# Two-chunk layout of gate and up weights, wider low-rank products, and a new order of the first rounds

## The chip, the cores and the metric

The kernel runs on one core of a Trainium2 chip. The metric is device microseconds of one execution. TensorE multiplies, VectorE, ScalarE and GpSimd do elementwise work, and SyncE (SP in the profile) issues most transfers from the chip's memory. The engines run their own instruction streams in order and meet at semaphores.

## The reference

Input x is 2 x 512 tokens of 512 features. What is computed, in four stages:

```
q, k, v = lin(x, Wq), lin(x, Wk), lin(x, Wv);  x1 = x + lin((q + k + v) / 3, Wo)
h = silu(lin(x1, Wgate)) * lin(x1, Wup)          # 1792 wide
x = layernorm(x + x1 + lin(h, Wdown))
x = layernorm(x + x @ W.T + low-rank)            # a 512 x 512 layer
x = layernorm(x + attention(x))                  # one head of 128
x = layernorm(x + expert mix(x))                 # 64 experts of rank 16, best 16 taken
```

Here lin(x, W) is x @ W.T plus a low-rank product x @ A.T @ B.T of rank 16. The weights of the first two stages come as 4-bit codes with a scale for each block of 64, and are looked up in a table of 16 values.

## The kernel before

**Weights.** The codes are read in 62 chunks of 128 x 512 (CHUNKS). For each chunk ScalarE and VectorE evaluate the table as a maximum and minimum of straight lines: `low` (two ScalarE passes into `bent` and a PSUM bank, one VectorE pass), `mid` (one and one), `clip` (VectorE), `out` (ScalarE L856 or L834, then VectorE into `value`, then GpSimd multiplies by the scale into `wf`, L745). TensorE makes the low-rank product A.T @ B.T of the chunk (the function `lora`), VectorE adds it to `wf` (`merge`, L1418 or L1415), and `split` writes the chunk as a high part rounded to the matmul type (ScalarE, `gu_hi` or `wd_hi`, L826) and a low part with what is left (GpSimd, `gu_lo` or `wd_lo`, L786).

**Products.** Every matrix product is made of three matmuls: high x high, high x low, low x high (`product`, L1056). A unit is one gate or one up product of 512 tokens with a chunk of 128 outputs: four k-steps of three matmuls, twelve in all.

**Rounds.** The 1792 hidden features are 14 rounds f of 128. A round has gate and up for each half of the tokens (units 2f and 2f + 1), then the products with the down chunk, which are made for pairs of rounds and spread over later rounds. The chunks g, u and d of round f + 1 are prepared during round f; in rounds 6, 8, 10 and 12 a chunk of the next stage's layer (an f chunk) is prepared as well. `silu`, `h` (the product with up, on VectorE), and `hsplit` (high part on ScalarE, low part on GpSimd) follow each unit.

**Order.** The order of the vector engines' work is one list, `vector_order`, and each of VectorE, ScalarE and GpSimd walks it and does its own share. From round 2 on it is made by a loop with the table BEATS; before that it is written out. TensorE's order is another list, `tensor_order`; in round f it is gate, down, up, down for the first half and the same for the second, with the `lora` of coming chunks between. A `lora` waits until the merge of the chunk before it has been done, since all use one PSUM bank.

**Gate and up chunks before.** Chunk g of a round holds the gate weights for all 512 input rows, chunk u those of up. `unit` waits for the chunk that it uses, once, before its twelve matmuls. The low-rank product of a chunk is four matmuls of 128 columns, one for each 128 input rows (L1069).

**Low-rank factors.** They are stacked three times over the partitions, and `bprep` rewrites a part of the stack as low parts: ScalarE picks rows (`chosen`, L830), GpSimd subtracts (L774). Part 0 is the A side; parts 1 and 2 are the B side for rounds 0 to 3 and 4 to 13. `dprep` does the same for the down chunks, `fprep` for the f chunks. The DMA of the B side is issued by SyncE with the attention chunks, between the codes.

Of the kernel before, what the change touches and what calls it, by code (L numbers as in the profile page):

```python
# [24 lines left out]
P = 128  # L25
# [81 lines left out]

BEATS = {0: [0] * 8, 4: [1, 0, 1, 0, 1, 0, 1, 0], 6: [1, 0, 1, 1, 2, 0, 1, 0], 8: [2, 0, 2, 0, 2, 0, 2, 0]}

# [21 lines left out]
RING_LN = 4  # L131
LB_FIRST = 4
XSPLIT_AFTER = [6, 7, 8, 9, 11, 12, 13, 14]


def vector_order():
# [67 lines left out]
    alone(("g", 1), 0)  # L204
    order.append(("x1", 0))
    alone(("g", 1), 1)
    order += [("merge", ("g", 0)), ("split", ("g", 0)), ("x1", 1), ("x1", 2), ("x1", 3)]
    order += [("merge", ("u", 0)), ("split", ("u", 0))]
    alone(("u", 1), 0)
    order.append(("x1", 4))  # L210
    alone(("u", 1), 1)
    order += [("merge", ("g", 1)), ("x1", 5), ("split", ("g", 1))]
    alone(("d", 0), 0)
    order.append(("x1", 6))
    alone(("d", 0), 1)
    order += [("merge", ("u", 1)), ("x1", 7)]
    alone(("d", 1), 0)
    order += [("split", ("u", 1)), ("dprep", 0)]
    alone(("d", 1), 1)
    order.append(("silu", 0))  # L220
    unit_h(0)
    half(("g", 2), 0)
    order += [("merge", ("d", 0)), ("split", ("d", 0)), ("bprep", 2), ("silu", 1)]
    unit_h(1)
    half(("g", 2), 1)
    order += [("merge", ("d", 1)), ("split", ("d", 1))]
    for f in range(1, NF):
        downs = downs_beside(f) + [None] * 4
        ahead = [(m, f + 1) for m in "gud" if (f, m) != (1, "g")] if f < NF - 1 else []
# [105 lines left out]
def build(nc, codes, scales, scales_qkv, eye, stack_low, xT, loA_o, loB_o, loA_qkv, loB_qkv, loA_gu, loB_gu,  # L335
          loA_d, loB_d, loA_f, loB_f, w_qkv, b_qkv, w_o, b_o, ex_A, ex_B, w_r, out):
    with ExitStack() as ctx:
# [32 lines left out]
        rows = at("rows", 98, [P, TT, H])  # L370
        bgu_raw = at("bgu_raw", 98, [P, FF])
        agu_raw = at("agu_raw", 105, [P, 2, 512])
        wq_hi = at("wq_hi", 146, [P, KT, H], F32R)
# [4 lines left out]
        wd_lo = at("wd_lo", 124, [P, RING_H, H], F32R)  # L378
        la_gu = at("la_gu", 134, [P, 2, 512], F32R)
        x1_hi = at("x1_hi", 146, [P, KT, TOK], F32R)  # L380
        x1_lo = at("x1_lo", 162, [P, KT, TOK], F32R)
        gu_hi = at("gu_hi", 178, [P, RING_GU, 2, KT, P], F32R)
        gu_lo = at("gu_lo", 186, [P, RING_GU, 2, KT, P], F32R)
# [4 lines left out]
        lb_gu = at("lb_gu", 194, [P, FF], F32R)  # L388
        la_d = at("la_d", 30, [P, FF // 2])
        la_dp = at("la_dp", 94, [P, FF // 2], F32R)  # L390
# [6 lines left out]
        half_eye = at("half_eye", 202.5, [P, P])  # L397
        three_eye = at("three_eye", 138, [P, P])

# [193 lines left out]

        def lb_cut(i):
            return slice(0, LB_FIRST * P) if i == 1 else slice(LB_FIRST * P, FF)

# [26 lines left out]
        def dest(c):  # L623

            kind, k = c
            if kind in "gu":
                g = "gu".index(kind)
                return gu_hi[:, k % RING_GU, g, :, :], gu_lo[:, k % RING_GU, g, :, :]
            if kind == "d":
                return wd_hi[:, k % RING_H, :], wd_lo[:, k % RING_H, :]  # L630
            return wff_hi[:, k, :], wff_lo[:, k, :]

        def shaped(c, w):
            return w.rearrange("p (k o) -> p k o", k=KT) if c[0] in "gu" else w

# [23 lines left out]
        def _(sp):  # L659
# [3 lines left out]
            for j, c in enumerate(CHUNKS):  # L663
# [3 lines left out]
                if c == ("v", 1):  # L667
                    sp.dma_start(bgu_raw[:, :], loB_gu).then_inc(bgu_in, 16)
                    sp.dma_start(agu_raw[:, :, :], loA_gu).then_inc(agu_in, 16)
                if c == ("q", 3):  # L670
                    sp.dma_start(xs[:, :, SEQ:], xT[:, :, SEQ:]).then_inc(x_in, 16)
                if c == ("k", 2):
                    sp.dma_start(la_d[:, :], loA_d).then_inc(lorad_in, 16)
                    sp.dma_start(lb_d[:, :, :], loB_d).then_inc(lorad_in, 16)
                    sp.dma_start(low_rows[:, 1:6], stack_low).then_inc(lorad_in, 16)
                if c == ("g", 3):
                    sp.wait_ge(x1_ready, NB * KT)
                    sp.dma_start(la_f[:, :], loA_f).then_inc(loraf_in, 16)
                    sp.dma_start(lb_f[:, :], loB_f).then_inc(loraf_in, 16)
# [37 lines left out]
        def _(pool):  # L717
# [7 lines left out]
            for item in filter(None, V):  # L725
# [41 lines left out]
                elif kind == "bprep":  # L767
                    i = item[1]
                    pool.wait_ge(bprep_hi, i + 1)
                    if i == 0:  # L770
                        lo, raw = la_gu[:, :, :], agu_raw[:, :, :]
                    else:
                        lo, raw = lb_gu[:, lb_cut(i)], bgu_raw[:, lb_cut(i)]
                    pool.tensor_tensor(lo, raw, lo.bitcast(F32), ALU.subtract).then_inc(bprep_done, 1)  # L774
                elif kind == "dprep":
# [48 lines left out]
        def _(act):  # L824
# [14 lines left out]
            for item in filter(None, V):  # L839
# [65 lines left out]
                elif kind == "bprep":  # L905

                    i = item[1]
                    act.wait_ge(bgu_in, 16)
                    act.wait_ge(agu_in, 16)
                    act.wait_ge(lorad_in, 48)  # L910
                    if i == 0:
                        chosen(la_gu[:, :, :], agu_raw[:, :, :], low_rows[:, 4:5], bprep_hi)
                    else:
                        cut = lb_cut(i)
                        chosen(lb_gu[:, cut], bgu_raw[:, cut], low_rows[:, 5:6], bprep_hi)
                elif kind == "dprep":
# [11 lines left out]
                elif kind == "down" and not item[1]:  # L928
                    t = item[2]
                    act.wait_ge(down_ready, t + 1)  # L930
                    act.wait_ge(bprep_done, 3)
                    copy(rows[:, t, :], down_bank(0, t)[:, :], down_added)
                elif kind == "silu":
                    n = item[1]
                    act.wait_ge(gate_ready, n + 1)
                    if n == 0:
                        act.wait_ge(dprep_done, 1)
                    if n >= 2:
# [111 lines left out]
        def _(pe):  # L1050
# [9 lines left out]
            def lora(c):  # L1060
# [84 lines left out]
            for n in range(KT, NB * KT):  # L1145
# [465 lines left out]
def laid_out(a):  # L1611
# [11 lines left out]
    for kind, k in CHUNKS:  # L1623
# [6 lines left out]
        elif kind in "gu":  # L1630
            g = "gu".index(kind)
            codes.append(cg[g][cut].reshape(P, KT, P).transpose(2, 1, 0).reshape(P, H))
            scales.append(sg[g][cut].reshape(P, KT, 2).transpose(2, 1, 0).reshape(2, H))
# [66 lines left out]
```

## Time and profile before

| | |
|---|---|
| median of three runs | 529.33 us (527.44 to 530.64) |
| profiled execution | 527.05 us, of which its span is 525.2 us |
| busy share of the span | TensorE 93%, VectorE 70%, ScalarE 56%, GpSimd 51% |
| mean granted clock of TensorE | 0.997 of full |
| gate and up products | 672 matmuls, 89.4 + 88.0 + 87.9 us busy |
| low-rank products of g and u chunks | 112 matmuls, 15.9 us busy |

Busy times of matmuls overlap, since one starts before the one ahead has ended; what a matmul costs is the step from its start to the start of the next. A row of the timeline has start, duration, engine, line, operation, what is written and read, shape and count, and in brackets how long the engine had been idle and what ended that. PE is TensorE's matmuls, PEld its weight loads, DVE VectorE, ACT ScalarE, POOL GpSimd.

### The profile page before, as it was taken

How to read it: one execution, taken by the hardware profiler on the slowest of the kernel's cores; microseconds unless marked ns; L12 is line 12 of the kernel's file. 1: busy time of each engine (PE TensorE's matmuls, PEld its weight loads, DVE VectorE, ACT ScalarE, POOL GpSimd, SP SyncE). 2: the span in 40 equal slices, each digit the busy share in tenths (PEclk: the TensorE clock that was granted, in tenths of full speed). 3: DMA queues.
4: the chain of work that ended last, by engine and by line, in shares of the span. 5: the costliest groups of instructions: out<-in, count | busy, mean ns of one | idle time of the engine just before them, and what ended most of it. 6: DMA issues, size and time to landing. Idle time of an engine off the chain costs nothing.

```text
span 525.2 us, 7548 instructions
## 1 busy us (share of the span) xinstructions
PE 485.9 (93%) x2272; PEld 392.1 (75%) x2272; DVE 366.1 (70%) x704; ACT 293.7 (56%) x542; POOL 267.1 (51%) x261
## 2 busy tenths in 40 slices
PE   2479889889999999999999999899998899999996
PEld 1246578668878888888888888688886688888884
DVE  5989878655458787997997974577457866366433
ACT  6989757655666566574765742158487422333021
POOL 4787726954446666575765653247479410110001
PEclk9999999989999999999999999999999999999999
DMA  8674412422223243343342300740000000000011
GB/s 208 227 246 138 136 60 85 137 81 81 61 80 101 81 121 100 102 108 93 109 126 72 117 1 3 267 162 1 1 1 1 2 0 22 21 20 21 1 41 40
DMA packets 21416, 43.01 MB, mean 82 GB/s; under 512 B 3329, under 2 KB 3457, under 8 KB 21121
## 3 DMA queue, kind: packets, MB, share of 16 engines
q1 hardware_dynamic: 21152, 42.16, 25.5%
q0 software_dynamic: 224, 0.38, 0.4%
q8 instruction: 19, 0.31, 0.2%
q14 instruction: 21, 0.16, 0.1%
HBM read 40.42 MB, written 2.10 MB: 81 GB/s over the span
## 4 chain that ended last, share of the span: by engine, by line
PE 76%; issue 6%; ACT 5%; DVE 5%; POOL 2%; DVEq 0%; ACTq 0%
PE bank L1056 66%; PE bank L1211 3%; PE bank L1069 2%; PE bank L1315 1%; PE bank L1116 1%; POOL gu_lo L786 1%; ACT bent L834 1%; PE bank L1104 1%; ACT prob L1012 1%; DVE wf L1418 1%; DVE value L1394 1%; PE bank L1194 1%; ACT bank L834 1%; PE bank L1078 1%; PE bank L1113 0%
## 5 line engine op out<-in xcount | busy, mean ns | idle before, releaser
L745 POOL TENSOR_TENSOR wf<-value,scale 128x512 f32<-128x512 f32 x50 | 64.5, 1291 | 73.7 <-DVE value L1394 70.4
L1056 PE MATMUL bank<-x_hi,gu_hi 128*128 128x512 f32 x224 | 89.4, 399 | 2.7 <-POOL gu_lo L786 2.7
L1056 PE MATMUL bank<-x_lo,gu_hi 128*128 128x512 f32 x224 | 88.0, 393 | 0.0
L1056 PE MATMUL bank<-x_hi,gu_lo 128*128 128x512 f32 x224 | 87.9, 392 | 0.0
L809 POOL TENSOR_TENSOR rstd<-veps,neg_half 128x1 f32<-128x1 f32 x32 | 17.6, 550 | 120.8 <-issue 109.6
L834 ACT ACTIVATE bank<-code 128x512 f32<-128x512 int32 x124 | 68.7, 586 | 0.0
L1372 DVE SCALAR_TENSOR_TENSOR low<-bent,bank 128x512 f32<-128x512 f32 x62 | 42.4, 684 | 25.5 <-ACT bank L834 22.1
L792 POOL TENSOR_TENSOR h_lo<-act_f,h_hi 128x512 fp32r<-128x512 f32 x28 | 36.5, 1302 | 36.3 <-ACT h_hi L826 36.3
L1056 PEld LDWEIGHTS bank<-x_hi,gu_hi 128*128 128x128 f32 x224 | 42.5, 190 | 11.5 <-issue 3.5
L1056 PEld LDWEIGHTS bank<-x_hi,gu_lo 128*128 128x128 f32 x224 | 42.5, 190 | 9.1
L1056 PEld LDWEIGHTS bank<-x_lo,gu_hi 128*128 128x128 f32 x224 | 42.5, 190 | 8.0
L1385 DVE SCALAR_TENSOR_TENSOR low<-low,bank 128x512 f32<-128x512 f32 x62 | 42.6, 687 | 5.7
L1056 PE MATMUL bank<-wd_hi,h_hi 128*128 128x512 f32 x112 | 44.9, 401 | 1.6 <-DVE rows L1461 1.6
L1378 DVE SCALAR_TENSOR_TENSOR bank<-code,bank 128x512 f32<-128x512 int32 x62 | 42.6, 687 | 5.1 <-ACT bank L856 4.7
L826 ACT ACTIVATE h_hi<-act_f 128x512 fp32r<-128x512 f32 x28 | 17.7, 631 | 50.9 <-DVE act_f L1454 45.5
L1056 PE MATMUL bank<-wd_hi,h_lo 128*128 128x512 f32 x112 | 43.8, 391 | 0.0
L1056 PE MATMUL bank<-wd_lo,h_hi 128*128 128x512 f32 x112 | 43.7, 390 | 0.0
L1461 DVE TENSOR_TENSOR rows<-bank,rows 128x512 f32<-128x512 f32 x40 | 27.6, 689 | 21.5 <-PE bank L1056 21.2
L1394 DVE SCALAR_TENSOR_TENSOR value<-bank,low 128x512 f32<-128x512 f32 x62 | 42.4, 684 | 0.1
L834 ACT ACTIVATE bent<-code 128x512 f32<-128x512 int32 x62 | 38.4, 620 | 3.7 <-DMA code<-codes 3.7
L786 POOL TENSOR_TENSOR gu_lo<-wf,gu_hi 128x512 fp32r<-128x512 f32 x28 | 36.3, 1296 | 4.5 <-ACT gu_hi L826 4.2
L856 ACT ACTIVATE bank<-code 128x512 f32<-128x512 int32 x62 | 36.7, 591 | 2.6 <-DVE low L1385 2.6
(202 smaller groups left out, 1152.0 us busy)
## 6 DMA issues: line engine op xcount, KB each, us to landing
code<-codes SPq DMA_DIRECT2D x62, 256.0 KB, 2.7
scale<-scales SPq DMA_DIRECT2D x100, 128.0 KB, 3.0
xs<-xT SPq DMA_DIRECT2D x2, 1024.0 KB, 6.0
ea_raw<-ex_A SPq DMA_DIRECT2D x1, 2048.0 KB, 10.0
eb_raw<-ex_B SPq DMA_DIRECT2D x1, 2048.0 KB, 7.6
out<-rows SPq DMA_DIRECT2D x8, 256.0 KB, 2.0
bgu_raw<-loB_gu SPq DMA_DIRECT2D x1, 896.0 KB, 5.9
wqkv_raw<-w_qkv SPq DMA_DIRECT2D x1, 768.0 KB, 4.3
```

The costliest lines, as they stand in the source:

```text
L745: pool.tensor_tensor(w, v, scale[:, i % RING_CODES, :], ALU.mult).then_inc(scaled_done, 1)
L786: pool.tensor_tensor(lo, shaped(c, w), hi.bitcast(F32), ALU.subtract).then_inc(lo_done, 1)
L792: pool.tensor_tensor(h_lo[:, f % RING_H, hs], act_f[:, n % 2, :], h_hi[:, f % RING_H, hs].bitcast(F32), ALU.subtract).then_inc(hlo_done, 1)
L826: nc.scalar.activation(dst, src, ACT.Copy).then_inc(done, 1)
L834: nc.scalar.activation(dst, src, ACT.Prelu, bias=float(start), scale=float(slope), alpha=float(alpha)).then_inc(done, 1)
L856: nc.scalar.activation(mid_ps[:, :], code[:, j % RING_CODES, :], ACT.Relu, bias=float(RELU_MID[1]), scale=float(RELU_MID[0])).then_inc(mid ...
L1056: last = nc.tensor.matmul(ps, a, b, start=start and i == 0 and n == 0, stop=stop and i == len(terms) - 1 and n == 2)
L1372: nc.vector.scalar_tensor_tensor(low[:, j % 2, :], bent[:, j % 2, :], float(BEND_LOW[3] - BEND_LAST[3]), last_ps[:, :], ALU.add, ALU.min). ...
L1378: nc.vector.scalar_tensor_tensor(mid_ps[:, :], code[:, j % RING_CODES, :], float(CODE_SHIFT), mid_ps[:, :], ALU.add, ALU.max).then_inc(mid ...
L1385: nc.vector.scalar_tensor_tensor(lj, lj, float(BEND_LAST[3]), mid_ps[:, :], ALU.add, ALU.min)\
L1394: nc.vector.scalar_tensor_tensor(value[:, j % 2, :], top_ps[:, :], float(BEND_TOP[3]), low[:, j % 2, :], ALU.add, ALU.max).then_inc(value_ ...
L1461: nc.vector.tensor_tensor(rows[:, t, :], down_bank(gi, t)[:, :], rows[:, t, :], ALU.add)\
```

## The change

A gate/up chunk now holds gate and up side by side, for half of the input rows: chunk g of a round has k-steps 0 and 1 of both, chunk u k-steps 2 and 3. A unit waits for both chunks, the second one after half of its matmuls. With the B side of gate and up side by side (and zero where the other's rows stand), one low-rank matmul makes 256 columns, both outputs of one k-step, and a chunk takes two instead of four. The A side has half the columns and the B side twice as many, so it comes in two transfers and is prepared in four parts; the parts use a buffer of their own for the rounded values. Some buffers move (`la_d` no longer shares room with `act_f`, and a wait of the first `silu` for `dprep` goes). The written-out order of the rounds 0 and 1 and of the second half of x1 is changed; the loop from round 2 on stays, and so does `tensor_order`. TensorE makes the low-rank product of ("g", 1) and ("u", 1) one x1 product later.

```
-BEATS = {0: [0] * 8, 4: [1, 0, 1, 0, 1, 0, 1, 0], 6: ..., 8: ...}
+BEATS = {0: [0] * 8, 6: ..., 8: ...}
-LB_FIRST = 4
+LB_PARTS = [(0, 4), (4, 7), (7, 11), (11, NF)]
+LB_HALF = 7
...
     order += [("bprep", 1), ("m1", KT - 1)]
     alone(("g", 1), 0)
-    order.append(("x1", 0))
+    order += [("x1", 0), ("x1", 1)]
     alone(("g", 1), 1)
-    order += [("merge", ("g", 0)), ("split", ("g", 0)), ("x1", 1), ("x1", 2), ("x1", 3)]
-    order += [("merge", ("u", 0)), ("split", ("u", 0))]
+    order += [("merge", ("g", 0)), ("x1", 2), ("split", ("g", 0)), ("x1", 3), ("merge", ("u", 0)), ("split", ("u", 0))]
     alone(("u", 1), 0)
-    order.append(("x1", 4))
+    order += [("bprep", 2), ("x1", 4)]
     alone(("u", 1), 1)
-    order += [("merge", ("g", 1)), ("x1", 5), ("split", ("g", 1))]
+    order += [("merge", ("g", 1)), ("x1", 5), ("bprep", 3), ("split", ("g", 1))]
     alone(("d", 0), 0)
     order.append(("x1", 6))
     alone(("d", 0), 1)
-    order += [("merge", ("u", 1)), ("x1", 7)]
-    alone(("d", 1), 0)
-    order += [("split", ("u", 1)), ("dprep", 0)]
-    alone(("d", 1), 1)
+    order += [("merge", ("u", 1)), ("x1", 7), ("dprep", 0), ("split", ("u", 1))]
+    alone(("d", 1))
+    order.append(("bprep", 4))
     order.append(("silu", 0))
-    unit_h(0)
-    half(("g", 2), 0)
-    order += [("merge", ("d", 0)), ("split", ("d", 0)), ("bprep", 2), ("silu", 1)]
-    unit_h(1)
-    half(("g", 2), 1)
-    order += [("merge", ("d", 1)), ("split", ("d", 1))]
-    for f in range(1, NF):
+    alone(("g", 2), 0)
+    order += [("h", 0), ("hsplit", 0)]
+    alone(("g", 2), 1)
+    order.append(("silu", 1))
+    alone(("u", 2), 0)
+    order += [("merge", ("d", 0)), ("split", ("d", 0)), ("h", 1), ("hsplit", 1)]
+    alone(("u", 2), 1)
+    order += [("merge", ("d", 1)), ("silu", 2), ("split", ("d", 1))]
+    alone(("d", 2), 0)
+    order += [("merge", ("g", 2)), ("split", ("g", 2)), ("h", 2), ("hsplit", 2)]
+    half(("d", 2), 1)
+    order += [("merge", ("u", 2)), ("silu", 3), ("split", ("u", 2))]
+    unit_h(3)
+    for f in range(2, NF):
...
                 if c == ("v", 1):
-                    sp.dma_start(bgu_raw[:, :], loB_gu).then_inc(bgu_in, 16)
-                    sp.dma_start(agu_raw[:, :, :], loA_gu).then_inc(agu_in, 16)
+                    sp.dma_start(agu_raw[:, :], loA_gu).then_inc(agu_in, 16)
+                    sp.dma_start(bgu_raw[0][:, :, :, :], loB_gu[:, :LB_HALF, :, :]).then_inc(bgu_in, 16)
...
+                if c == ("v", 3):
+                    sp.dma_start(bgu_raw[1][:, :, :, :], loB_gu[:, LB_HALF:, :, :]).then_inc(bgu_in, 16)
...
                 elif kind == "bprep":
...
-                        chosen(lb_gu[:, cut], bgu_raw[:, cut], low_rows[:, 5:6], bprep_hi)
+                        act.wait_ge(bprep_done, i)
+                        chosen(lb_part(i)[2], lb_part(i)[1], low_rows[:, 5:6], bprep_hi)
...
-                    if n == 0:
-                        act.wait_ge(dprep_done, 1)
...
-                    pe.wait_ge(bprep_done, 2 if k < LB_FIRST else 3)
-                    for h in range(KT):
-                        last = nc.tensor.matmul(lora_ps[:, h * P:(h + 1) * P],
-                                                la_gu[:, "gu".index(kind), h * P:(h + 1) * P],
-                                                lb_gu[:, k * P:(k + 1) * P], start=True, stop=True)
+                    pe.wait_ge(bprep_done, 2 + next(i for i, (a, b) in enumerate(LB_PARTS) if a <= k < b))
+                    for h in range(2):
+                        m = 2 * "gu".index(kind) + h
+                        last = nc.tensor.matmul(lora_ps[:, 2 * h * P:2 * (h + 1) * P], la_gu[:, m * P:(m + 1) * P],
+                                                lb_gu[k // LB_HALF][:, k % LB_HALF, :, :], start=True, stop=True)
...
-                if r in (0, 2):
-                    lora((("g", 1), ("u", 1))[r // 2])
+                if r in (1, 2):
+                    lora((("g", 1), ("u", 1))[r - 1])
...
-                pe.wait_ge(hi_done, split_no(("gu"[g], f)))
-                pe.wait_ge(lo_done, split_no(("gu"[g], f)))
                 s, ps = f % RING_GU, unit_ps[m % 3][:, :]
-                product(ps, [(gu_hi[:, s, g, k, :], gu_lo[:, s, g, k, :], x1_hi[:, k, tk], x1_lo[:, k, tk])
-                             for k in range(KT)]).then_inc((gate_ready, unit_ready)[g], 1)
+                for h in range(2):
+                    pe.wait_ge(hi_done, split_no(("gu"[h], f)))
+                    pe.wait_ge(lo_done, split_no(("gu"[h], f)))
+                    last = product(ps, [(gu_hi[:, s, k, g, :], gu_lo[:, s, k, g, :], x1_hi[:, k, tk], x1_lo[:, k, tk])
+                                        for k in (2 * h, 2 * h + 1)], start=h == 0, stop=h == 1)
+                last.then_inc((gate_ready, unit_ready)[g], 1)
```

## Rows read from the trace of the kernel before

**Rows 1.** Busy time by stretch: first rounds, rounds; then clock, DMA share, GB/s.
```profile
core 0: us, PE busy (x) PEld busy (x) DVE busy (x) ACT busy (x) POOL busy (x), PEclk, DMA share, GB/s
64.00:116.00 52.00, 45.69 (x206) 36.73 (x207) 37.93 (x61) 33.95 (x61) 33.03 (x24) 0.99 0.28 87
116.00:314.00 198.00, 197.19 (x921) 163.83 (x921) 154.09 (x243) 122.74 (x229) 121.00 (x94) 0.99 0.31 91
```

**Rows 2.** What TensorE waited for: total us, times, longest.
```profile
PE bank L1069 <- DVE wf L1418: 2.8, 2, 1.6
PE bank L1056 <- POOL gu_lo L786: 2.7, 2, 1.9
...
PE bank L1069 <- DVE wf L1415: 0.6, 1, 0.6
...
PE bank L1078 <- POOL lb_dp L780: 0.5, 1, 0.5
```

**Rows 3.** Timeline of TensorE's matmuls around one low-rank group.
```profile
66.36 0.39 PE L1056 MATMUL bank<-x_hi,m_lo 128*128 128x512 f32 x1
66.59 0.56 PE L1069 MATMUL bank<-lb_gu,la_gu 128*128 128x128 f32 x4
66.98 0.45 PE L1056 MATMUL bank<-x_hi,m_hi 128*128 128x512 f32 x1
67.27 0.40 PE L1056 MATMUL bank<-x_lo,m_hi 128*128 128x512 f32 x1
```

**Rows 4.** Timeline of TensorE's weight loads behind that group.
```profile
66.92 0.19 PEld L1056 LDWEIGHTS bank<-x_hi,m_hi 128*128 128x128 f32 x1
67.03 0.19 PEld L1056 LDWEIGHTS bank<-x_lo,m_hi 128*128 128x128 f32 x1
```

**Rows 5.** Timeline, start of round 3: gate, ScalarE's copy and high part, u's low part.
```profile
131.56 0.39 PE L1056 MATMUL bank<-x_hi,gu_hi 128*128 128x512 f32 x1
...
131.76 0.60 ACT L826 ACTIVATE rows<-bank 128x512 f32<-128x512 f32 x1 [2.88 <-PE bank L1056]
...
133.30 0.62 ACT L826 ACTIVATE gu_hi<-wf 128x512 fp32r<-128x512 f32 x1
...
134.72 1.30 POOL L786 TENSOR_TENSOR gu_lo<-wf,gu_hi 128x512 fp32r<-128x512 f32 x1
```

**Rows 6.** Timeline, round 4: gate's start, u's low part, up's start.
```profile
150.93 0.39 PE L1056 MATMUL bank<-x_hi,gu_hi 128*128 128x512 f32 x1
...
155.26 1.27 POOL L786 TENSOR_TENSOR gu_lo<-wf,gu_hi 128x512 fp32r<-128x512 f32 x1
...
156.68 0.47 PE L1056 MATMUL bank<-x_hi,gu_hi 128*128 128x512 f32 x1 [0.81 <-POOL gu_lo L786]
```

**Rows 7.** Timeline, round 5: gate's start, u's low part.
```profile
169.96 0.39 PE L1056 MATMUL bank<-x_hi,gu_hi 128*128 128x512 f32 x1
...
171.55 1.30 POOL L786 TENSOR_TENSOR gu_lo<-wf,gu_hi 128x512 fp32r<-128x512 f32 x1
```

**Rows 8.** Timeline, rounds 7 and 8: u's low part and gate's start in each.
```profile
201.38 1.29 POOL L786 TENSOR_TENSOR gu_lo<-wf,gu_hi 128x512 fp32r<-128x512 f32 x1
...
205.16 0.39 PE L1056 MATMUL bank<-x_hi,gu_hi 128*128 128x512 f32 x1
...
223.11 0.39 PE L1056 MATMUL bank<-x_hi,gu_hi 128*128 128x512 f32 x1
...
224.85 1.30 POOL L786 TENSOR_TENSOR gu_lo<-wf,gu_hi 128x512 fp32r<-128x512 f32 x1
```

**Rows 9.** The view of rows 1 for the stretch behind the 1.9 us wait.
```profile
115.50:118.80 3.30, 3.30 (x9) 2.53 (x9) 1.25 (x3) 0.32 (x1) 1.28 (x1) 0.50 0.28 82
```

**Rows 10.** Timeline: clip of g2, merge of d0, then the low-rank product of d1.
```profile
92.48 0.69 DVE L1385 SCALAR_TENSOR_TENSOR low<-low,bank 128x512 f32<-128x512 f32 x1
93.36 0.69 DVE L1415 SCALAR_TENSOR_TENSOR wf<-wf,bank 128x512 f32<-128x512 f32 x1 [0.19 <-PE bank L1078]
...
95.86 0.39 PE L1078 MATMUL bank<-lb_dp,la_dp 128*128 128x512 f32 x1
```

**Rows 11.** Preparation of the B side: GpSimd's two instructions (ns: shortest, median, longest); its DMA.
```profile
L774 POOL TENSOR_TENSOR lb_gu<-bgu_raw,lb_gu x2: 1286/2122/2957, 64.2 to 96.4; 128x512 fp32r<-128x512 f32 x1, 128x1280 fp32r<-128x1280 f32 x1
...
DMA to landing us min/median/max: 5.9/5.9/5.9
```

More of the change, by code:

```diff
@@ L104 @@
 FFN_AT = {6: 0, 8: 1, 10: 2, 12: 3}
-BEATS = {0: [0] * 8, 4: [1, 0, 1, 0, 1, 0, 1, 0], 6: [1, 0, 1, 1, 2, 0, 1, 0], 8: [2, 0, 2, 0, 2, 0, 2, 0]}
+BEATS = {0: [0] * 8, 6: [1, 0, 1, 1, 2, 0, 1, 0], 8: [2, 0, 2, 0, 2, 0, 2, 0]}
 def chunk_list():
@@ L215, in vector_order @@
     alone(("d", 0), 1)
-    order += [("merge", ("u", 1)), ("x1", 7)]
-    alone(("d", 1), 0)
-    order += [("split", ("u", 1)), ("dprep", 0)]
-    alone(("d", 1), 1)
+    order += [("merge", ("u", 1)), ("x1", 7), ("dprep", 0), ("split", ("u", 1))]
+    alone(("d", 1))
+    order.append(("bprep", 4))
     order.append(("silu", 0))
-    unit_h(0)
-    half(("g", 2), 0)
-    order += [("merge", ("d", 0)), ("split", ("d", 0)), ("bprep", 2), ("silu", 1)]
-    unit_h(1)
-    half(("g", 2), 1)
-    order += [("merge", ("d", 1)), ("split", ("d", 1))]
-    for f in range(1, NF):
+    alone(("g", 2), 0)
[12 more added lines that the diff above has]
+    for f in range(2, NF):
         downs = downs_beside(f) + [None] * 4
-        ahead = [(m, f + 1) for m in "gud" if (f, m) != (1, "g")] if f < NF - 1 else []
+        ahead = [(m, f + 1) for m in "gud"] if f < NF - 1 else []
         ahead += [("f", FFN_AT[f])] if f in FFN_AT else []
@@ L370, in build @@
         rows = at("rows", 98, [P, TT, H])
-        bgu_raw = at("bgu_raw", 98, [P, FF])
-        agu_raw = at("agu_raw", 105, [P, 2, 512])
+        agu_raw = at("agu_raw", 98, [P, 512])
         wq_hi = at("wq_hi", 146, [P, KT, H], F32R)
@@ L378, in build @@
         wd_lo = at("wd_lo", 124, [P, RING_H, H], F32R)
-        la_gu = at("la_gu", 134, [P, 2, 512], F32R)
+        la_gu = at("la_gu", 134, [P, 512], F32R)
         x1_hi = at("x1_hi", 146, [P, KT, TOK], F32R)
         x1_lo = at("x1_lo", 162, [P, KT, TOK], F32R)
-        gu_hi = at("gu_hi", 178, [P, RING_GU, 2, KT, P], F32R)
-        gu_lo = at("gu_lo", 186, [P, RING_GU, 2, KT, P], F32R)
+        gu_hi = at("gu_hi", 178, [P, RING_GU, KT, 2, P], F32R)
+        gu_lo = at("gu_lo", 186, [P, RING_GU, KT, 2, P], F32R)
         la_o = at("la_o", 182, [RANK, 512])
@@ L387, in build @@
         lb_qkv = at("lb_qkv", 192, [3 * RANK, 512])
-        lb_gu = at("lb_gu", 194, [P, FF], F32R)
-        la_d = at("la_d", 30, [P, FF // 2])
+        lb_gu = [at("lb_gu0", 194, [P, LB_HALF, 2, P], F32R), at("lb_gu1", 136, [P, LB_HALF, 2, P], F32R)]
+        bgu_raw = [at("bgu_raw0", 194, [P, LB_HALF, 2, P]), at("bgu_raw1", 136, [P, LB_HALF, 2, P])]
+        bgu_hi = at("bgu_hi", 102, [P, 4, 2, P], F32R)
+        la_d = at("la_d", 120, [P, FF // 2])
         la_dp = at("la_dp", 94, [P, FF // 2], F32R)
@@ L397, in build @@
         half_eye = at("half_eye", 202.5, [P, P])
-        three_eye = at("three_eye", 138, [P, P])
+        three_eye = at("three_eye", 143.5, [P, P])
         la_f = at("la_f", 90, [P, 512])
@@ L592, in down_bank, with lb_part @@
             return bank[7] if gi < len(GROUPS) - 1 else bank[7 - t % 2]
-        def lb_cut(i):
-            return slice(0, LB_FIRST * P) if i == 1 else slice(LB_FIRST * P, FF)
+        def lb_part(i):
+            a, b = LB_PARTS[i - 1]
+            n = a // LB_HALF
+            cut = slice(a - n * LB_HALF, b - n * LB_HALF)
+            return lb_gu[n][:, cut, :, :], bgu_raw[n][:, cut, :, :], bgu_hi[:, 0:b - a, :, :]
         def slot_free_down(f):
@@ L626, in dest @@
             if kind in "gu":
-                g = "gu".index(kind)
-                return gu_hi[:, k % RING_GU, g, :, :], gu_lo[:, k % RING_GU, g, :, :]
+                half = slice(2 * "gu".index(kind), 2 * "gu".index(kind) + 2)
+                return gu_hi[:, k % RING_GU, half, :, :], gu_lo[:, k % RING_GU, half, :, :]
             if kind == "d":
@@ L633, in shaped @@
         def shaped(c, w):
-            return w.rearrange("p (k o) -> p k o", k=KT) if c[0] in "gu" else w
+            return w.rearrange("p (k g o) -> p k g o", k=2, g=2) if c[0] in "gu" else w
         def late_weights():
@@ L770, in _ @@
                     if i == 0:
-                        lo, raw = la_gu[:, :, :], agu_raw[:, :, :]
+                        dst, raw, hi = la_gu[:, :], agu_raw[:, :], la_gu[:, :]
                     else:
-                        lo, raw = lb_gu[:, lb_cut(i)], bgu_raw[:, lb_cut(i)]
-                    pool.tensor_tensor(lo, raw, lo.bitcast(F32), ALU.subtract).then_inc(bprep_done, 1)
+                        dst, raw, hi = lb_part(i)
+                    pool.tensor_tensor(dst, raw, hi.bitcast(F32), ALU.subtract).then_inc(bprep_done, 1)
                 elif kind == "dprep":
@@ L907, in _ @@
                     i = item[1]
-                    act.wait_ge(bgu_in, 16)
+                    act.wait_ge(bgu_in, 16 if i < 3 else 32)
                     act.wait_ge(agu_in, 16)
@@ L911, in _ @@
                     if i == 0:
-                        chosen(la_gu[:, :, :], agu_raw[:, :, :], low_rows[:, 4:5], bprep_hi)
+                        chosen(la_gu[:, :], agu_raw[:, :], low_rows[:, 4:5], bprep_hi)
                     else:
-                        cut = lb_cut(i)
-                        chosen(lb_gu[:, cut], bgu_raw[:, cut], low_rows[:, 5:6], bprep_hi)
+                        act.wait_ge(bprep_done, i)
+                        chosen(lb_part(i)[2], lb_part(i)[1], low_rows[:, 5:6], bprep_hi)
                 elif kind == "dprep":
@@ L930, in _ @@
                     act.wait_ge(down_ready, t + 1)
-                    act.wait_ge(bprep_done, 3)
+                    act.wait_ge(bprep_done, 1 + len(LB_PARTS))
                     copy(rows[:, t, :], down_bank(0, t)[:, :], down_added)
@@ L1630, in laid_out @@
         elif kind in "gu":
-            g = "gu".index(kind)
-            codes.append(cg[g][cut].reshape(P, KT, P).transpose(2, 1, 0).reshape(P, H))
-            scales.append(sg[g][cut].reshape(P, KT, 2).transpose(2, 1, 0).reshape(2, H))
+            half = slice(2 * "gu".index(kind), 2 * "gu".index(kind) + 2)
+            codes.append(cg[:, cut].reshape(2, P, KT, P).transpose(3, 2, 0, 1)[:, half].reshape(P, H))
+            scales.append(sg[:, cut].reshape(2, P, KT, 2).transpose(3, 2, 0, 1)[:, half].reshape(2, H))
         elif kind == "d":
@@ L1647, in laid_out @@
     Ba, Bg, Bd = (np.asarray(a[n]) for n in ("L0_attn_lora_B_attn", "L0_attn_lora_B_gu", "L0_attn_lora_B_down"))
-    la_gu = np.zeros((P, 2, 512), np.float32)
-    lb_gu = np.zeros((P, FF), np.float32)
+    la_gu = np.zeros((P, 512), np.float32)
+    lb_gu = np.zeros((P, NF, 2, P), np.float32)
     for i in range(3):
@@ L1652, in laid_out @@
             r = 32 * i + RANK * g
-            la_gu[r:r + RANK, g] = Ah[4 + g]
-            lb_gu[r:r + RANK] = Bg[g].T
+            la_gu[r:r + RANK] = Ah[4 + g]
+            lb_gu[r:r + RANK, :, g] = Bg[g].T.reshape(RANK, NF, P)
     la_d = np.zeros((P, FF // 2), np.float32)
```

## The prediction

> **What bounds the kernel now.** I read the busy times by stage first, then what TensorE waits for, then the timeline around those waits. While the gate/up/down rounds run (116 to 314 us) TensorE is busy 197.19 of 198.00 us; just before, in the first rounds (64 to 116 us), only 45.69 of 52.00 [rows 1]. So in the rounds a microsecond added to or taken from TensorE's queue moves the end by a microsecond, whether it is work or a wait. The waits of TensorE are few: in the first rounds 2.8 + 0.6 us on merges (L1418, L1415), 0.5 us on `lb_dp`, and 2.7 us in two waits for `gu_lo` [rows 2], which are `up` of round 2 (1.9 us) and of round 4 (0.8 us). The reader should see that in the rounds the other engines are just in time or late by little, not far ahead: what counts is when a gate/up chunk's low part lands against when TensorE first asks for it.
>
> **Low-rank products: removed.** A gate or up chunk now takes four products of 128 columns. A plain product starts 0.227 us after the one before (66.36 to 66.59). The four start at 66.59; the next product starts at 66.98 and the one behind it at 67.27, where without the four it would have been 66.82: the group costs 0.45 us, not 0.39, because the next weight load is late too [rows 3]. Weight loads that wait for nothing else follow each other by 0.11 us (66.92, 67.03), so four loads alone fill the 0.45 [rows 4]. After the change there are two loads and two products of 256 columns. No row shows 256 columns. From below the loads give 2 x 0.11 = 0.22 us; from above a 512-column product gives 2 x 0.227 = 0.45 us, no saving. By columns 256 is half of 0.227, 0.114, which is close to the load pitch, so I take 0.23. Saving: 28 chunks x 0.22 = 6.2 us, bounds 0 and 6.4, all on TensorE's queue.
>
> The Trainium skill (TensorE: Matmul & The Clock Gate, Back-to-back issue gap) gives an isolated gap of columns / 2.4 GHz plus 2.5 ns, which speaks against this change: four of 128 would take about 0.22 us and two of 256 the same, a saving of nothing. The trace's 0.45 us for the four does not agree. The same page's rule for loads (LDWEIGHTS, columns / 1.2 GHz, 0.107 us) does agree with the 0.11 us.
>
> **Gate waits for the second chunk: added.** So far gate of round f needs chunk g alone, and chunk u is asked for by `up`, some 4 us later. Now each chunk holds both outputs for half of the input rows, so the last six of gate's twelve products need u's low part. They would start 6 x 0.227 = 1.36 us after gate starts. The order of the vector engines from round 3 on is not touched, nor is TensorE's order. In it the split of u for round f stands behind `hsplit` of the last unit of round f-1, and in rounds 2 and 3 behind the copy of that round's third `down` too. So u's low part is tied to TensorE's own progress just ahead of gate, and no lead won earlier helps. What the trace shows for each round, with 0.14 us from the end of the low part to the product that waits (155.26 + 1.27 = 156.53, product at 156.68):
> - Round 3: gate starts 131.56, its seventh product would at 132.92; ScalarE copies the `down` (131.76), finishes u's high part (133.30 + 0.62), and GpSimd the low part at 134.72 + 1.30 = 136.02 [rows 5]. Wait 3.1 + 0.14 = 3.2 us.
> - Round 4: gate 150.93, seventh 152.29, low part 156.53 (the two `fprep` copies stand in the same stretch): wait 4.4 us. The wait of `up`, 0.8 us, goes in return [rows 6].
> - Rounds 5 and 6: 169.96, seventh 171.32, low part 172.85 [rows 7]: 1.7 us; round 6 repeats it at about 1.5.
> - Rounds 8, 10 and 12: 223.11, seventh 224.47, low part 226.15 [rows 8]: 1.8 us each.
> - Rounds 7, 9, 11 and 13: the round ahead also prepares an `f` chunk, the halves come sooner, and the low part (201.38 + 1.29) is there before gate starts at 205.16 [rows 8]: nothing.
>
> Sum 3.2 + 4.4 + 1.7 + 1.5 + 3 x 1.8 = 16.2, less 0.8 = 15.4. In rounds 8 to 12 a merge that delays the last h will be done earlier when TensorE is late; I take 15.0. Nothing hides it: TensorE's queue is in order and has no other idle time there.
>
> **First rounds in another order: moved.** The waits listed above come to 1.6 + 0.5 + 0.6 + 1.2 + 1.9 = 5.8 us, and behind the last one TensorE's clock was granted at half, 1.2 GHz, in all of the 3.3 us that follow [rows 9], which costs 1.7 us: 7.5 us in all. I walked the new order item by item with the durations of rows (VectorE 0.69, ScalarE 0.60 to 0.62, GpSimd 1.30 us a pass [rows 5, 10]). Better: g2 and u2 are prepared sooner, u2's low part lands around 111.4 us, before gate of round 2 gets to its second half, so the 1.9 us and the half clock go. Worse: the merge of d0 now stands behind a whole further chunk. Before, it follows the clip of g2 directly (92.48, then 93.36), and the low-rank product of d1 at 95.86 has no wait [rows 10]. Now h0, its split, low of u2, value of g2, silu 1, mid and clip of u2 come between, a ping-pong of ScalarE and VectorE of some 5.3 us; with the 2 us that the stream has gained by then, the merge ends near 97.4. TensorE ends `up` of the second unit near 93.5 and stands until then: 3.9 us. Behind this product are all of round 1's. The others I find: 0.9 us for u0's product, now behind g0's later merge, 1.3 for g2's, 0.45 for u2's. New sum 6.6 us: a gain of 1.0, bounds a gain of 7.5 (every wait gone) and a loss of 1.7 (another half-clock stretch).
>
> **Preparation of the low-rank factors.** One pair is 512 columns instead of 1024, the four others cover 3584 instead of 1792. GpSimd takes 1.29 us for 512 and 2.96 for 1280 columns [rows 11]: about 11 us against 6.6 before, in an engine with 33 of 52 us busy [rows 1]; it is inside the walk above. The DMA for the second half (896 KB; the same size took 5.9 us [rows 11]) is queued on SyncE ahead of the codes of the last attention chunk; that chunk is read some 5 us after its issue, so I take 0, at most 1 us. TensorE's second pair of waits in each unit costs nothing where it is met, since sequencer waits run ahead of the products.
>
> **Clock.** One idle stretch of 1.9 us was followed by half clock, one of 1.6 us was not [rows 2, 9]. The two of 3.2 and 4.4 us lie beyond both. Each costs between 0 (the half-clock time falls into the idle) and 1.7; I take 1.1 each, 2.2.
>
> **Sum.** -6.2 + 15.0 - 1.0 + 2.2 = +10.0 us. The profiled execution took 527.05 us (span 525.2); the median of the runs, 529.33, is 2.3 above it. So 537.1 for an execution like the profiled one, and 539.3 as a median.
>
> **Rivals.**
> - *More half clock* (chance 0.14): the 3.9 us in round 1 and some of the five shorter waits also drop the clock, four stretches more at 1.7: +7, 546. For: 1.9 us was enough. Against: 1.6 us was not, and five of the waits lie at 1.5 to 1.8. The Trainium skill (TensorE: Matmul & The Clock Gate, HAM oscillation) has idle gaps throttle the array again and again; the trace has one such case.
> - *The products don't shrink* (0.12): 256 columns cost what 512 do; the 6.2 us are not saved, 545.5.
> - *All first-round waits go* (0.12): if the merge of d0 ends before `up` of the second unit does (about 93.5 us), no wait is left there. Gain 7.5 instead of 1.0: 532.8.
> - *The second half comes in time, faster* (0.06): if u's low part lands within 1.36 us of gate's start in every round, as it does in rounds 7, 9, 11 and 13, the 15.0 and the 2.2 vanish and 522.1 is left. It needs the split of u to run ahead of the last h of the round before. Rounds 5 to 12 speak against it: ScalarE's split follows `h_hi` in the same queue.
>
> **How the numbers follow.** My forecast has 0.56. The range reaches from below the case without first-round waits, with room for less half clock (531.5), to the two dearer cases (546.5). Half a per cent, 2.6 us, is about what a measurement can tell from no change: 526.7 to 532.0 is "same". Slower: the forecast, the two dear rivals, and half of the first-round case, 0.88. Same: the rest of that case and a little of the last, 0.07. Faster 0.05.
>
> **What would show it.** The waits of TensorE on `gu_lo` rise from 2.7 us in two places to about 16 in seven or eight, inside gate, in rounds 3, 4, 5, 6, 8, 10, 12 and not in 7, 9, 11, 13. The low-rank line has 56 products instead of 112, and the product behind a group starts about 0.23 us late. A wait of about 4 us stands before the low-rank product of d1, and none at round 2's `up`. Half clock after the long waits. It is wrong if TensorE has no idle time inside gate from round 3 on, or if a group of two still takes 0.45 us.

## The result and the profile after

The changed kernel takes 547.4 us (median of four runs, 546.2 to 549.4), the kernel before 529.4 us beside it: a ratio of 1.035 [1.031, 1.039], 18.0 us slower. The forecast was 539.3, with 546.5 as the upper end of the range. The profiled execution of the changed kernel took 547.9 us (span 546.1).

What TensorE waited for after, in the view of [rows 2]:

```profile
PE bank L1066 <- POOL gu_lo L798: 16.7, 7, 4.2
...
PE bank L1088 <- DVE wf L1427: 3.4, 1, 3.4
...
PE bank L1080 <- DVE wf L1430: 1.5, 2, 0.8
```

The wait for `gu_lo` has gone from 2.7 us in two places to 16.7 us in seven. These are the seven on TensorE's timeline, each ahead of the seventh product of a gate:

```profile
135.82 0.77 PE L1066 MATMUL bank<-x_hi,gu_hi 128*128 128x512 f32 x1 [3.02 <-POOL gu_lo L798]
...
162.02 0.52 PE L1066 MATMUL bank<-x_hi,gu_hi 128*128 128x512 f32 x1 [4.19 <-POOL gu_lo L798]
...
183.84 0.47 PE L1066 MATMUL bank<-x_hi,gu_hi 128*128 128x512 f32 x1 [2.16 <-POOL gu_lo L798]
...
202.94 0.47 PE L1066 MATMUL bank<-x_hi,gu_hi 128*128 128x512 f32 x1 [1.54 <-POOL gu_lo L798]
...
240.18 0.47 PE L1066 MATMUL bank<-x_hi,gu_hi 128*128 128x512 f32 x1 [1.93 <-POOL gu_lo L798]
...
279.04 0.47 PE L1066 MATMUL bank<-x_hi,gu_hi 128*128 128x512 f32 x1 [1.94 <-POOL gu_lo L798]
...
316.30 0.47 PE L1066 MATMUL bank<-x_hi,gu_hi 128*128 128x512 f32 x1 [1.94 <-POOL gu_lo L798]
```

They are rounds 3, 4, 5, 6, 8, 10 and 12. Round 3 on all engines (compare [rows 5]): gate starts at 131.27, ScalarE copies a `down`, then makes the last h's high part and u's high part, GpSimd follows with the two low parts, and the seventh product starts 0.15 us after u's low part has landed (134.41 + 1.26):

```profile
131.27 0.39 PE L1066 MATMUL bank<-x_hi,gu_hi 128*128 128x512 f32 x1
...
131.47 0.60 ACT L838 ACTIVATE rows<-bank 128x512 f32<-128x512 f32 x1 [2.36 <-PE bank L1066]
...
132.49 0.62 ACT L838 ACTIVATE h_hi<-act_f 128x512 fp32r<-128x512 f32 x1
...
133.01 0.62 ACT L838 ACTIVATE gu_hi<-wf 128x512 fp32r<-128x512 f32 x1
...
133.19 1.27 POOL L804 TENSOR_TENSOR h_lo<-act_f,h_hi 128x512 fp32r<-128x512 f32 x1 [1.84 <-ACT h_hi L838]
...
134.41 1.26 POOL L798 TENSOR_TENSOR gu_lo<-wf,gu_hi 128x512 fp32r<-128x512 f32 x1
```

Busy times by stretch (the columns of [rows 1]): the first rounds, the rounds, and the four stretches at half clock. Before, there was one such stretch of 3.3 us [rows 9].

```profile
64.00:116.00 52.00, 45.64 (x193) 36.51 (x192) 36.87 (x60) 34.07 (x60) 37.17 (x26) 0.93 0.31 91
97.40:104.30 6.90, 5.60 (x13) 4.49 (x14) 3.73 (x6) 2.71 (x5) 5.00 (x4) 0.51 0.65 193
116.00:314.00 198.00, 183.05 (x802) 147.95 (x800) 139.54 (x221) 114.97 (x216) 109.44 (x86) 0.97 0.31 87
135.00:141.80 6.80, 5.98 (x16) 4.85 (x17) 0.00 (x0) 0.60 (x1) 0.67 (x1) 0.50 0.01 2
162.30:165.70 3.40, 3.40 (x12) 2.67 (x10) 0.00 (x0) 0.60 (x1) 0.00 (x0) 0.50 0.00 0
240.80:244.20 3.40, 3.40 (x10) 2.62 (x9) 0.13 (x1) 1.62 (x4) 0.90 (x1) 0.50 0.46 126
```

In such a stretch a 512-column product follows the one before it after 0.43 us (99.29 to 99.72, below) instead of 0.23, so nearly half of the busy time is lost: at most 3.0 + 1.7 + 1.7 = 6.4 us in the rounds, 2.8 in round 1. In round 1 the merge of d0 (VectorE, ends 98.65) is late for the low-rank product of d1, as the prediction walked it (against [rows 10]):

```profile
97.97 0.68 DVE L1427 SCALAR_TENSOR_TENSOR wf<-wf,bank 128x512 f32<-128x512 f32 x1
...
98.70 0.80 PE L1088 MATMUL bank<-lb_dp,la_dp 128*128 128x512 f32 x1 [3.40 <-DVE wf L1427]
99.29 0.63 PE L1066 MATMUL bank<-x_hi,gu_hi 128*128 128x512 f32 x1
99.72 0.63 PE L1066 MATMUL bank<-x_lo,gu_hi 128*128 128x512 f32 x1
```

The low-rank group itself, against [rows 3]: two products of 256 columns start at 281.86, the next product at 282.09 and the one behind it 0.24 us later. The group takes 0.23 to 0.24 us, where it took 0.45; so do most of the 28 (20 take 0.24 to 0.25):

```profile
281.86 0.40 PE L1080 MATMUL bank<-lb_gu,la_gu 128*128 128x256 f32 x2
282.09 0.40 PE L1066 MATMUL bank<-x_hi,gu_hi 128*128 128x512 f32 x1
282.33 0.40 PE L1066 MATMUL bank<-x_lo,gu_hi 128*128 128x512 f32 x1
```

Laid against each other product by product, the two profiled executions differ by 20.9 us at the end. 1.7 us of it arise at the start, ahead of any changed code. The first rounds give 2.0 us back by the start of round 3. From there to the last `down` product it is 236.4 us against 215.1, 21.3 us more: the seven waits and the half-clock stretches behind three of them. What follows the last `down` product takes the same time in both, within 0.1 us.

### The profile page after: what moved, and what is told of

It reads as the page before. It is cut to its first block and busy times, and to the rows that moved or that the text cites. A ratio compares the mean times of both kernels' runs of the same rounds, so it can differ in the third digit from the quotient of the medians.

```text
span 546.1 us, 7502 instructions
## 1 busy us (share of the span) xinstructions
PE 491.8 (90%) x2216; PEld 392.0 (72%) x2216; DVE 365.4 (67%) x704; ACT 295.1 (54%) x544; POOL 270.3 (49%) x263
## 5 line engine op out<-in xcount | busy, mean ns | idle before, releaser
L1066 PE MATMUL bank<-x_hi,gu_hi 128*128 128x512 f32 x224 | 90.1, 402 | 16.7 <-POOL gu_lo L798 16.7
L1066 PE MATMUL bank<-x_lo,gu_hi 128*128 128x512 f32 x224 | 89.6, 400 | 0.0
L1066 PE MATMUL bank<-x_hi,gu_lo 128*128 128x512 f32 x224 | 89.4, 399 | 0.0
L846 ACT ACTIVATE bank<-code 128x512 f32<-128x512 int32 x124 | 68.6, 586 | 0.0
L1066 PE MATMUL bank<-wd_hi,h_hi 128*128 128x512 f32 x112 | 46.0, 411 | 1.6 <-DVE rows L1473 1.6
L950 ACT ACTIVATE act_f<-bank 128x512 f32<-128x512 f32 x28 | 16.6, 592 | 43.6 <-PE bank L1066 43.1
```

Of the source, the lines that this page charges most:

```text
L846: nc.scalar.activation(dst, src, ACT.Prelu, bias=float(start), scale=float(slope), alpha=float(alpha)).then_inc(done, 1)
L1066: last = nc.tensor.matmul(ps, a, b, start=start and i == 0 and n == 0, stop=stop and i == len(terms) - 1 and n == 2)
```

## The experiments

The question is which of the four terms (products, gate waits, first rounds, clock) missed, since the waits are where they were expected. The theory: the gate waits and the half clock behind them are the loss. The rivals: the first rounds, or products that save nothing.

**The wait alone, in the kernel before.** Gate's second half also waits for chunk u; nothing else is changed.

```
-product(ps, [... for k in range(KT)])
+for h in range(2):
+    if h == 1 and g == 0:
+        pe.wait_ge(hi_done, split_no(("u", f)))
+        pe.wait_ge(lo_done, split_no(("u", f)))
+    last = product(ps, [... for k in (2 * h, 2 * h + 1)], start=h == 0, stop=h == 1)
```

> The kernel before, with one thing of the change: gate's seventh matmul waits for chunk u of its round as well. Theory 1 (gate's wait on the second chunk makes the loss, and the half clock behind the longer waits adds to it): from the timeline of before the waits are 3.7 us in round 2 (in place of 1.9 of up), 3.2, 4.4 (in place of 0.8), 1.7, 1.5 and three of 1.8, together 17 us net, and some 4 us of half clock: about 550 us. Rival (the new order of the first rounds and the preparation make it): at most 535 us. Rival (the wait is paid back later, other engines catch up): at most 535 us too, with waits of TensorE in gate in the profile.

549.8 us, ratio 1.039 [1.035, 1.043]. Its waits of TensorE:

```profile
PE bank L1056 <- POOL gu_lo L786: 18.9, 8, 4.2
```

So asking for chunk u six gate and six `down` products sooner (12 x 0.227 = 2.7 us) costs 20.1 us by itself, all of the loss and more, half clock and round 2's longer wait included.

**Two products of 256 columns, in the kernel before.** The low-rank values added to the weights are not the reference's here: the columns lie as the kernel before has them.

```
-for h in range(KT):
-    last = nc.tensor.matmul(lora_ps[:, h * P:(h + 1) * P], ..., lb_gu[:, k * P:(k + 1) * P], ...)
+for h in range(2):
+    last = nc.tensor.matmul(lora_ps[:, 2 * h * P:2 * (h + 1) * P], ..., lb_gu[:, at_col:at_col + 2 * P], ...)
```

> The kernel before, with two low-rank matmuls of 256 columns in place of four of 128 for each g and u chunk; the values of the low-rank part are not the reference's, nothing else is changed. My prediction has 0.22 us less for a group, 28 x 0.22 = 6.2 us: 523.2 us. From the steps between rounds in the profile of the changed kernel a group is only 0.15 us cheaper: 4.2 us, 525.2. If a product of 256 columns costs what one of 512 does: 529.4, no change.

526.6 us, ratio 0.993 [0.991, 0.996]: 3.5 us saved by the ratio (3.2 by the medians), not 6.2. In the trace each of the ten groups of rounds 2 to 6 saves about 0.20 us; at four later points the lead shrinks again, by 0.14 to 0.34 us each.

**Gate's first half made twice** in the seven rounds with a wait (changed kernel; the idle time is filled with products whose result is made again).

```
+if g == 0 and b == 0 and f in (3, 4, 5, 6, 8, 10, 12):
+    product(ps, [... for k in range(2)])
```

> The changed kernel; in the seven rounds in which gate waits, its first six matmuls are made twice (the first time for nothing), so that TensorE is idle 1.4 us less in each and the second half starts when it did. Theory 1a (half clock comes from the length of the idle stretch): with idle stretches of 1.6, 2.8, 0.8, 0.2 and three of 0.6 us in place of 3.0, 4.2, 2.2, 1.5 and 1.9 the half clock in the rounds goes, some 5 to 6 us: 541 to 542 us. Rival (half clock has another cause, or costs nothing since it falls into idle time): 547 us. If the added matmuls were on the path in rounds: over 547 us.

541.8 us, ratio 1.025 [1.020, 1.029], though TensorE makes 42 products more (42 x 0.227 = 9.5 us):

```profile
PE bank L1066 <- POOL gu_lo L798: 7.4, 7, 2.8
```

The idle time fell by 9.3 us, which the extra products took up; no half-clock stretch is left in the rounds. In the profiles, the time from the start of round 3 to the last `down` product is 230.7 us against 236.4: 5.7 us are the price of the 13.6 us at half clock there. The medians differ by 5.6, but there round 1 has a part too: its half-clock stretch is 3.4 us long in this profile and 6.8 in the changed kernel's.

**The split of u early** (changed kernel): behind its own merge from round 3 on, not behind the last h of the round before.

```
+for k in range(3, NF):
+    order.remove(("split", ("u", k)))
+    order.insert(order.index(("merge", ("u", k))) + 1, ("split", ("u", k)))
```

> The changed kernel; in the order list the split of u from round 3 on stands right behind its merge, ahead of the last h of the round before and its hsplit. Theory 1: u's low part is then there when gate gets to its second half, the seven waits (16.7 us) and the half clock behind them (some 6 us) go: 547.4 - 22 = 525 us. Rival (the vector engines can't have it sooner, or hsplit, 0.6 and 1.3 us later, holds up down products or the next silu): waits of TensorE of the same size on h_lo or on act_f, 540 us or more. If only half of the waits go: about 536 us.

526.2 us, ratio 0.994 [0.992, 0.996]: 21.2 us less than the changed kernel, and 0.6% less than the kernel before. The long waits are gone; round 1's stays, and with it a stretch at half clock from 99.5 to 106.3:

```profile
PE bank L1091 <- DVE wf L1430: 3.4, 1, 3.4
...
PE bank L1069 <- POOL gu_lo L801: 1.2, 5, 0.4
```

**The merges of round 1 early.** On top of the early split, d0 is merged behind the clip of g2, as in the kernel before, and d1, g2 and u2 follow sooner.

```
-order += [("h", 0), ("hsplit", 0)]
+order += [("merge", ("d", 0)), ("h", 0), ("hsplit", 0), ("split", ("d", 0))]
 alone(("g", 2), 1)
-order.append(("silu", 1))
+order += [("merge", ("d", 1)), ("silu", 1), ("split", ("d", 1))]
...
```

> The kernel of split_early with the new order kept, but the merges of d0 and d1 in round 1 moved up (d0's right behind the clip of g2, as in the kernel before, d1's behind the middle of that chunk's preparation), and those of g2 and u2 one unit earlier. Theory (the 3.4 us wait at the low-rank product of d1 and the 6.8 us of half clock behind it come of d0's late merge): that wait falls under 1 us, the half-clock stretch near 99 us goes, and the time is 526.2 - 3.4 - 2.4 = about 520.5 us (519 to 523). Rival (the vector engines have no room there, the wait only moves on to the low-rank product of g2 or u2): the waits of the first rounds still sum to 4 us or more and the time stays at 525 to 527.5.

521.6 us, ratio 0.986 [0.983, 0.989], the fastest version of the study. No wait for d0's merge is left, nor a half-clock stretch in the first rounds (granted clock 1.00 from 64 to 116 us):

```profile
64.00:116.00 52.00, 50.01 (x223) 39.91 (x224) 40.66 (x65) 36.43 (x66) 38.79 (x27) 1.00 0.32 92
```

The same merges in the changed kernel itself, its split of u left where it is:

> The changed kernel with only the merges of d0, d1, g2 and u2 moved up, as in d_early; the split of u stays where the changed kernel has it. It tells whether the 3.4 us wait and the half clock of round 1 are part of the 18 us, or are taken back by the later waits. Theory (they add, as d_early stands to split_early, -4.6 us): 547.4 - 4.6 = 542.8 us, 541 to 544.5, with the seven waits for u's low part still at 16 to 17.5 us. Rival (what is won ahead of round 2 is lost again at the waits): 546 to 549.

542.8 us, ratio 1.025 [1.022, 1.028]. The seven waits are the same 16.7 us, and the 4.6 us come in full. So the late merges of round 1, with the wait and the half clock behind that of d0, cost 4.6 of the changed kernel's 547.4; d0's alone was not moved in any run.

**The old order of the first rounds**, with the early split.

> The kernel of the run split_early (526.2 us; split of u right behind its merge), but with the first rounds in the order of the kernel before, the three later pairs of low-rank factors prepared behind the merges of d0 and d1. It tells what the new order of the first rounds is worth by itself. The ledger of the changed kernel had its first rounds some 0.2 us ahead of before's by round 3, of which its low-rank products account for 1.5, so the new order alone would cost about 1 us, its 3.4 us wait and 6.8 us of half clock included. Theory (the new order is worth about nothing): 524 to 527.5 us. Rival 1 (as I predicted, the new order gains 1 us or more): over 528. Rival 2 (the wait and the half clock of round 1 cost what they show, some 5 us, and the old order has neither): 521 to 523.

533.8 us, ratio 1.007 [1.005, 1.010]. Only the rival over 528 has the number, and not for its reason: here the three later pairs of low-rank factors are prepared behind the merges of d0 and d1, near where the kernel before prepares its last part, and ScalarE, which shares one buffer for the rounded values with GpSimd, stands in line behind GpSimd's passes. The clip and the merge of the next chunk are behind it; rows of ScalarE and TensorE:

```profile
107.04 0.94 ACT L840 ACTIVATE bgu_hi<-bgu_raw,low_rows 128x768 fp32r<-128x768 f32 x1 [3.73 <-POOL lb_gu L784]
...
112.01 0.58 PE L1078 MATMUL bank<-lb_gu,la_gu 128*128 128x256 f32 x1 [6.15 <-DVE wf L1428]
```

That run said nothing of the order. With the factors prepared where the changed kernel does it:

```
-order.append(("x1", 4))
+order += [("bprep", 2), ("x1", 4)]
...
-order += [("bprep", 3), ("merge", ("d", 1)), ("split", ("d", 1)), ("bprep", 4)]
+order += [("merge", ("d", 1)), ("split", ("d", 1))]
```

> The kernel of old_first with the three later pairs of low-rank factors prepared where the changed kernel prepares them (by the end of d1's preparation) and not behind the merges of d0 and d1. In old_first ScalarE stood 3.73 us (until 107.04) for GpSimd's passes over these factors, with the clip of the next chunk behind it, and TensorE then waited 6.1 us. Theory (that late preparation made old_first slow; the order of the merges itself is worth little): the 6.1 us wait and the half clock behind it go, 524 to 528 us, as split_early (526.2). Rival 1 (without d0's late merge the old order is the better one): 520 to 523, as d_early. Rival 2 (the order, not the preparation, made it slow): 530 or more.

526.2 us, ratio 0.994 [0.992, 0.996], the same as the early split with the new order. The new order by itself is worth nothing that the medians show; in the old order, the place of the preparation is worth 7.6 us.

**Four products of 128 columns again**, first in the kernel with the early split, then in the changed kernel.

```
-for h in range(2):
-    m = 2 * "gu".index(kind) + h
-    last = nc.tensor.matmul(lora_ps[:, 2 * h * P:2 * (h + 1) * P], ...)
+for h in range(KT):
+    m = 2 * "gu".index(kind) + h // 2
+    last = nc.tensor.matmul(lora_ps[:, h * P:(h + 1) * P], ...)
```

> The kernel of split_early with four low-rank products of 128 columns a chunk in place of two of 256 (the same results). It prices the products in the changed kernel. By my prediction, 28 x 0.22 = 6.2 us more: 532.4. Theory after two_products (0.19 us a group, part of which is given back where TensorE then waits for a merge): 3.5 to 5.3 us more, 529.6 to 531.5. Rival (the products cost the same): 526.2.

526.9 us, ratio 0.997 [0.994, 1.000], which is 0.7 us more by the medians and 1.7 by the ratios; the theory (3.5 to 5.3) missed.

> The changed kernel itself with four low-rank products of 128 columns a chunk in place of two of 256 (the same results), and nothing else. It prices the term that I put at 6.2 us in the kernel for which I predicted it. My prediction: 547.4 + 6.2 = 553.6. As in the kernel before (two_products, 3.5 us): 550.9 (549.5 to 552). As in the kernel with the early split (four_again, 0.7 to 1.7 us, where the vector engines' work takes most of the saving back): 548 to 549. In the changed kernel the seven waits start from TensorE's own last h, so that work won ahead of them should stay won: I expect the middle one.

545.5 us, ratio 1.030 [1.026, 1.033]: not slower than with two products, and my choice of the middle case fell. The waits and two of the gates of this kernel:

```profile
PE bank L1066 <- POOL gu_lo L798: 15.4, 7, 4.2
```

```profile
276.59 0.47 PE L1066 MATMUL bank<-x_hi,gu_hi 128*128 128x512 f32 x1 [1.68 <-POOL gu_lo L798]
...
313.96 0.47 PE L1066 MATMUL bank<-x_hi,gu_hi 128*128 128x512 f32 x1 [1.68 <-POOL gu_lo L798]
```

From round 10's wait to round 12's TensorE takes 37.37 us with four products and 37.26 with two (279.04 to 316.30 above), though four shorter groups lie between. With two products the wait is 0.26 us longer instead, and short waits for merges ahead of down chunks' low-rank products take most of the rest. What ends the wait can be read in both traces: the last product of `up` ahead of round 10, and VectorE's h of that unit, with two products and with four:

```profile
273.76 0.39 PE L1066 MATMUL bank<-x_hi,gu_lo 128*128 128x512 f32 x1
...
274.95 0.68 DVE L1466 SCALAR_TENSOR_TENSOR act_f<-bank,act_f 128x512 f32<-128x512 f32 x1
```

```profile
271.58 0.39 PE L1066 MATMUL bank<-x_hi,gu_lo 128*128 128x512 f32 x1
...
272.50 0.68 DVE L1466 SCALAR_TENSOR_TENSOR act_f<-bank,act_f 128x512 f32<-128x512 f32 x1
```

VectorE is not idle ahead of h in either (no bracket): `value` and `merge` of its list stand ahead of it, and h starts 1.19 us after that product with two products a group, 0.92 with four. The 0.27 us that TensorE is ahead are the 0.26 of longer wait.

Ahead of round 3 more is kept: from the first group to the start of round 3 it is 62.98 us with two products and 64.00 with four, 1.0 us. That the kernel with four is 1.9 us faster by the medians goes with the clock: its rounds hold one stretch of 6.8 us at half clock, the changed kernel's 13.6 us, and from round 3 to the last `down` product they take 233.9 us against 236.4. At 5.7 us for 13.6, the 6.8 us are worth 2.9; by this estimate two products save about 0.4 us in the rounds.

## Why the prediction was right or wrong

**Right: place and mechanism.** The waits stand in the seven rounds named and in no other, at 3.0, 4.2, 2.2, 1.5 and three times 1.9 us against 3.2, 4.4, 1.7, 1.5 and 1.8; less the 0.8 us of `up` in round 4, which went as forecast, 15.9 us net for the 15.0 of the sum. Round 2's `up` no longer waits. The wait at d1's low-rank product is 3.4 us for 3.9. The experiment with the wait alone and the one with the early split show from both sides that these waits decide.

**The step that failed: the low-rank saving as a term of its own.** The size of a group was right (0.45 to 0.23 us). The Trainium skill's isolated gap (TensorE: Matmul & The Clock Gate, Back-to-back issue gap), by which two products of 256 columns take about 0.22 us, agrees with the 0.23; by it four of 128 would take the same, and there the trace has 0.45. But "28 chunks x 0.22 = 6.2 us, all on TensorE's queue" holds only where TensorE does not wait later for something that comes no earlier. In the kernel before 3.5 us were kept, with the early split 0.7 to 1.7, in the changed kernel some 1.4 by the traces (1.0 ahead of round 3 and the estimated 0.4) and none that the medians show. I added a saving and a wait as though independent, having costed the wait from a trace with the longer groups: in the five waits from round 5 on, groups shorter by 0.2 us make the wait longer by 0.2 to 0.3; those of rounds 3 and 4 are 3.02 and 4.19 us with either. That the vector engines' list sets when the wait ends is shown by the rows of round 10; for the other rounds it is argued from the longer waits. The rival "the products don't shrink" had its time, 545.5, nearly right for another reason.

**Mis-sized: the clock.** I took 2.2 us for two stretches; the rounds lost 5.7 us (gate's first half made twice), in three. The stretch behind round 8's wait was not in my sum, and round 3's is 6.8 us long, twice that of [rows 9]. The rival with more half clock, 546, came nearest to the result and deserved more than 0.14.

**First rounds.** Predicted -1.0. Their lead of 2.0 us by round 3, less the 1.0 of the shorter groups, leaves -1.0, but the number is in part luck: the waits there come to 4.9 us (0.66 + 3.40 + 0.84) in place of 6.6 (none at g2's product, where 1.3 were forecast, and 0.84 for 0.45 at u2's), and the half clock behind the 3.4 us, up to 2.8 us, was in the bounds and not in the sum. (The bound itself is off: one more stretch of 1.7 turns a gain of 1.0 into a loss of 0.7. The preparation, put at about 11 us of GpSimd, is 9.8 in the trace and by the durations of [rows 11].) The 1.6 us wait at the low-rank product of ("g", 1) has gone; that product alone comes one x1 product later, the one of ("u", 1) stands where it stood. What I had not seen is that round 1's wait could be taken out for 4.6 us by moving four merges and their splits, and that the larger preparation is harmless only where the change puts it: put behind the merges of d0 and d1, it made the old order 7.6 us slower.

The sum by measured terms is -1.0 + 15.9 + 5.7 - 1.0 = 19.6 us, against 19.2 in the profiled executions after the 1.7 us at the start are taken off, and 18.0 by the medians. What lies between the last two may be clock, which differs from run to run: the mean granted clock of the four runs was 0.980 to 0.986.

## What to carry to other kernels

When two operands are repacked so that the first consumer needs both, look up when the second one was ready before: a load that was "in time" for its old reader can be late for the new one, and the cure is to move its preparation (here one line of the order, worth 21 us), not to drop the layout. A saving on an engine that goes on to wait for others is only kept up to that wait, so price waits in the schedule that the other edits leave. And an idle stretch has a second price in the clock behind it; a range should hold it for every wait of that length, not for the longest two.

## What the runs showed of the hardware

The same wait was not always followed by the half clock. In the changed kernel TensorE stood 3.02 us in round 3 and ran at 0.50 from 135.0 to 141.8; with four products it stood 3.02 us in the same round, until 136.00, and the same stretch was granted in full, while its round 4 was not (busy times and granted clock of that run, the columns of [rows 1]):

```profile
135.00:141.80 6.80, 5.80 (x27) 4.82 (x28) 0.38 (x1) 2.67 (x6) 0.85 (x1) 1.00 0.01 2
158.50:165.30 6.80, 5.47 (x15) 4.43 (x16) 0.24 (x1) 0.60 (x1) 1.18 (x1) 0.50 0.00 0
```

Within the changed kernel the wait of 1.93 us in round 8 was followed by 3.4 us at half clock, the two of 1.94 in rounds 10 and 12 by none. So the length of one idle stretch does not settle it in these runs; the half-clock stretches behind the waits were 3.4 or 6.8 us long. Filling part of the idle time took the stretches of the rounds away (gate's first half made twice). The Trainium skill has idle gaps throttle the array again (TensorE: Matmul & The Clock Gate, HAM oscillation), and these runs agree with it; which of several like gaps does so is not to be read from these rows.
